# A ViT tower on one core: second feed-forward layer in blocks of 128 tokens with shared left-overs, output product of chosen rows once per two groups

## The chip, the cores and the metric

The kernel runs on one core of a Trainium2 chip. The engines of the core each work through a queue of their own in order: TensorE (PE, whose weight loads are shown as PEld), VectorE (DVE), ScalarE (ACT), GpSimd (POOL) and SyncE (SP, which here only issues transfers). The metric is the device time in microseconds (us) of one execution; less is better. Times of the kernel before: 670.09 us, median of 3 runs (669.08 to 673.85).

## The reference

The input x has shape (64, 12, 224, 224). Three stages follow one another.

1. Tokens: every 16x16 patch of each channel is summed, which gives 14x14 = 196 tokens of 12 numbers per image; a 12x192 matrix maps them to 192 features (h).
2. Attention on layernorm(h): 12 heads of 16, a causal mask, an output projection. Only k_sel = ceil(sqrt(196)) = 14 tokens per image, those with the largest softmax selection score, get the attention output added (`y = x.at[idx].add(gated attention)`); all others pass the layer norm itself. The result is added to h.
3. Feed-forward on layernorm(h): `gelu(xt @ in_weight.T + in_bias) @ out_weight`, with 192 -> 768 -> 192, added to h. The output has shape (64, 196, 192) in f32.

Because the tokens have rank 12 plus a constant, the kernel works with 12 to 13 numbers per token in place of 192 wherever the algebra allows.

## The kernel before, in words

Images go in groups of 4 (GB), 16 groups (NG). A group has 4 x 196 = 784 tokens (GT) and 4 x 14 = 56 chosen rows (SLOTS). Every engine runs the same loop over periods: in a period each stage works on the group given by the period's number less the stage's lag. The order inside a period is written out by hand, one string `plan` per engine (PE lines 724 to 727, ScalarE 908 to 910, DVE 1247, GpSimd 469); an entry such as `o:6.1:2` reads "stage o, step 6.1, lag 2". No scheduler moves anything; semaphores named by `Steps` (lines 99 to 107) order the engines among each other.

The stages, in the order in which a group passes them:

- **L** (DVE, line 1055): seven tiles of x are summed in the free dimension. For two tiles GpSimd adds halves first (H, line 430), for one a DMA adds them (X, line 425). The sums go through DRAM (ScalarE issues the store `R:st`, line 847, and the load `R:ld`, line 852) and come back by channel; GpSimd adds the quarters (line 439).
- **A**: token statistics and the selection. PE makes token products (`tm`, line 585), DVE the first layer norm's scale (line 1065 and on), PE transposes (`zt`, line 591, and `sl`, line 596, the scores of selection), DVE finds the top 14 (line 1113 to 1131; the last of it writes `srow`), PE turns `srow` (`st`, line 600), DVE makes the one-hot matrix Sg (line 1137).
- **K**: GpSimd (lines 373 to 467), in turns with ScalarE (line 830), splits the tokens into bf16 parts; PE transposes them (`tr1`, `tr2`, line 613) and ScalarE copies them out of PSUM as two stacks, `Stk1` (line 836, step k1) and `Stk2` (line 841, step k2). The copies also reorder the tokens so that block i holds tokens i, i+7, i+14, ...: `by_tile` and `tokens_by_tile`, lines 341 to 347.
- **f**: the first feed-forward layer, twelve bf16 products of 392 columns through the one PSUM bank psF (PE line 700), each followed by a GELU on ScalarE (line 893) that must end before the next product starts.
- **o / O**: the second layer. Seven blocks (FT) of 112 tokens (OT) per group, each six f32 products of 192 columns and one bf16 product for the residual (PE lines 715 and 719; an f32 product is two MATMUL instructions in the trace), evicted by ScalarE (line 900). After block 6 ScalarE issues the group's store (line 903). Two banks, psO, take turns.
- **G**: PE gathers the chosen tokens (`ga`, lines 624 to 626), DVE masks them (ZY, line 1145), PE makes U and the residual rows (`u`, lines 632 and 637), DVE masks U into UB (line 1162).
- **S**: attention of the chosen rows. Scores (PE 647), row maxima (DVE 1169), exponentials (ScalarE 864), reciprocal (DVE 1175), normalisation (ScalarE 869), transpositions (PE 653, ScalarE 873), product with the tokens (PE 659), mask into G2 (DVE 1180), the output product `at` (PE line 670: six f32 products of G2, 56 columns, with B2, 192 columns, in three lots of two) and the new rows h1 (DVE 1190).
- **C**: once per two groups, on the 120 rows of h1 (56 of the even group, 56 of the odd one from row 64 on): layer norm, both feed-forward layers (PE 679 to 690, ScalarE 879 to 887, DVE 1196 to 1211); then GpSimd writes the chosen rows over their places in the output by an indirect store (line 450), after the group's plain store has landed.

The entries that matter for the change, in PE's order within a period: `K:tr1 o:4.0 o:4.1 K:tr2 f:0 at:0 A:sl at:1 o:4.2 f:1 at:2 f:2 o:5.0 f:3 A:st o:5.1 f:4 G:ga f:5 o:5.2 f:6 G:u f:7 o:6.0 C:xt f:8 o:6.1 C:fa f:9 S:sc f:10 o:6.2 f:11 C:fb A:tm o:0.0`. The C entries act only where the group of lag 2 is odd. ScalarE's order at the period's end is `f:10 O:6 f:11 C:gb S:e0 ... S:e5`, then, in the next period, `O:0 S:n A:fm`.

Of the kernel before, what the change touches and what calls it, by code (L numbers as in the profile page):

```python
# [7 lines left out]
T = N * N  # L8
HD = D // HEADS
KSEL = int(np.ceil(np.sqrt(T)))  # L10
GB = 4
NG = B // GB
# [24 lines left out]
FT = 7  # L37
FP = T // FT
OT = GB * FP
# [70 lines left out]
def program(nc, x, cw, wqkv, bqkv, selw, selb, ow, ob, temp, w1t, b1, w2, consts, e48, e13r, out):  # L110
# [4 lines left out]
    og = out.rearrange("(g b) (t i) e -> g (b t) (i e)", b=GB, i=FT)  # L115
# [4 lines left out]
    with ExitStack() as ctx:  # L120
# [54 lines left out]
        act_sb = [sb(f"act{i}", [128, HT, GT]) for i in range(2)]  # L175

# [5 lines left out]
        G2 = sb("G2", [128, HP, SLOTS])  # L182
        dsm, dsel = sb("dsm", [SLOTS, GB]), sb("dsel", [SLOTS, 1])
        base = sb("base", [SLOTS, 1])
        idx = [sb(f"idx{i}", [SLOTS, 1], i32) for i in range(4)]
        res = sb("res", [SLOTS, D])
# [5 lines left out]
        obuf = [sb(f"obuf{i}", [OT, FT, D]) for i in range(2)]  # L192

# [24 lines left out]
        y_out = [sem(f"out_stored{k}") for k in range(2)]  # L218
        scat = [sem(f"chosen_stored{k}") for k in range(2)]
# [22 lines left out]
        pe_S = Steps(sem("pe_attention"), "sc et g at")  # L242
        dve_S = Steps(sem("dve_attention"), "mx nm ri g0 g1 h1")
        act_S = Steps(sem("act_attention"), "e0 e1 e2 e3 e4 e5 n0 n1 n2 n3 n4 n5 t0 t1 t2")

# [4 lines left out]
        outs = " ".join(f"o{k}" for k in range(FT))  # L250
        pe_F1 = Steps(sem("pe_ffn1"), ffn)
        act_F1 = Steps(sem("act_gelu"), ffn)
# [88 lines left out]
        def by_tile(t):  # L341

            return t[:, :].rearrange("p (i m) -> p i m", i=FT)

        def tokens_by_tile(ap):

            return ap.rearrange("p (m i) -> p i m", i=FT)
# [37 lines left out]
        def _(sp):  # L385
# [29 lines left out]
            for r in range(2):  # L415
                sp.wait_ge(sums_out[r], landed(NG - 4 + r, r))
                sp.wait_ge(y_out[r], landed(NG - 2 + r, r))
                sp.wait_ge(scat[r], landed(NG - 2 + r, r))

        @block.gpsimd  # L420
        def _(pool):
# [79 lines left out]
        def _(pe):  # L501
# [115 lines left out]
            def step_G(g, u, name):  # L617
# [46 lines left out]
            def step_at(g, j):  # L664

                if j == 0:
                    pe.wait_ge(dve_S.sem, dve_S.at(g, "g1"))
                    if isinstance(g, int) and g < 2:
                        pe.wait_ge(dve_W.sem, dve_W.at(0, "ob"))
                mm = pe.matmul(psS[0:SLOTS, 0, 0:D], G2[:, j, :], B2[:, j, :], start=(j == 0), stop=(j == HP - 1))  # L670
                if j == HP - 1:
                    mm.then_inc(pe_S.sem, 1)
# [30 lines left out]
            def step_F2(g, u, i, m):  # L703

                to = psO[(i + u) % 2][0:OT, 0:D]
                if m == 0:
# [5 lines left out]
                    if exists(g if i >= 2 else g - 1):  # L712
                        pe.wait_ge(act_F2.sem, act_F2.at(g if i >= 2 else g - 1, f"o{(i - 2) % FT}"))
                if m < HT:
                    pe.matmul(to, act_sb[u % 2][:, m, i * OT:(i + 1) * OT], W2[:, m, :], start=(m == 0), stop=False)  # L715
                else:
                    if i == 0:
                        pe.wait_ge(act_K.sem, act_K.at(g, "k2"))
                    pe.matmul(to, Stk2[u % 2][:, i * OT:(i + 1) * OT], RS[:, :], start=False, stop=True).then_inc(pe_F2.sem, 1)  # L719
# [9 lines left out]
            def body(i, k):  # L729
                for what in first if isinstance(i, int) and k == 1 else plan:  # L730
# [11 lines left out]
                    elif stage == "o":  # L742
                        for m in {0: (0, 1), 1: (2, 3), 2: (4, 5, 6)}[int(step[2])]:
                            step_F2(g, u, int(step[0]), m)
                    elif stage == "f":
                        step_F1(g, u, int(step))
                    elif stage == "at":
                        step_at(g, 2 * int(step))
                        step_at(g, 2 * int(step) + 1)
                    else:  # L750
                        {"A": step_A, "G": step_G, "K": step_K, "S": step_S}[stage](g, u, step)
# [8 lines left out]
        def _(act):  # L760
# [24 lines left out]
            def first_group():  # L785
# [21 lines left out]
                for name in "HML":  # L807
                    step_K(0, 0, name)
# [15 lines left out]
            def step_K(g, u, name):  # L824
# [7 lines left out]
                elif name == "k1":  # L832
# [3 lines left out]
                    act.activation(by_tile(Stk1[u % 2]), tokens_by_tile(psA[:, :].bitcast(bf16)[0:SK, 0:GT]), ACT.Copy).then_inc(act_K.sem, 1)  # L836
                else:
                    act.wait_ge(pe_K.sem, pe_K.at(g, "tr2"))
                    if exists(g - 2):
                        act.wait_ge(pe_F2.sem, pe_F2.at(g - 2, f"o{FT - 1}"))  # L840
                    act.activation(by_tile(Stk2[u % 2]), tokens_by_tile(psA[:, :].bitcast(bf16)[0:SK, 0:GT]), ACT.Copy).then_inc(act_K.sem, 1)
# [12 lines left out]
            def step_G(g, u, name):  # L854

                act.wait_ge(pe_G.sem, pe_G.at(g, "rs"))
                act.activation(res[:, :], psS[0:SLOTS, 0, D:2 * D], ACT.Copy).then_inc(act_G.sem, 1)
# [38 lines left out]
            def step_F2(g, u, i):  # L896
                act.wait_ge(pe_F2.sem, pe_F2.at(g, f"o{i}"))
                if i == 0 and exists(g - 2):
                    act.wait_ge(y_out[u % 2], landed(g - 2, u % 2))
                act.activation(obuf[u % 2][:, i, :], psO[(i + u) % 2][0:OT, 0:D], ACT.Copy).then_inc(act_F2.sem, 1)  # L900
                if i == FT - 1:
                    act.wait_ge(act_F2.sem, act_F2.at(g, f"o{i}"))
                    act.dma_start(og[bass.ds(g, 1)].rearrange("o p q -> (o p) q"),
                                  obuf[u % 2][:, :, :].rearrange("p i e -> p (i e)")).then_inc(y_out[u % 2], 16)

            first = ("K:k1:1 K:k2:1 f:0:1 f:1:1 f:2:1 f:3:1 f:4:1 f:5:1 f:6:1 f:7:1 f:8:1 f:9:1 f:10:1 f:11:1 "
                     "O:0:1 G:rs:1 O:1:1 S:e0:1 S:e1:1 S:e2:1 S:e3:1 S:e4:1 S:e5:1").split()
            plan = ("O:0:2 S:n:2 A:fm:1 O:1:2 A:e:1 S:t:2 K:H:1 K:M:1 O:2:2 K:L:1 K:k1:1 R:st:0 K:k2:1 f:0:1 O:3:2 "
                    "f:1:1 f:2:1 O:4:2 f:3:1 f:4:1 R:ld:0 f:5:1 O:5:2 f:6:1 f:7:1 G:rs:1 C:XH:2 f:8:1 f:9:1 C:ga:2 "
                    "f:10:1 O:6:2 f:11:1 C:gb:2 S:e0:1 S:e1:1 S:e2:1 S:e3:1 S:e4:1 S:e5:1").split()  # L910

            def body(i, k):
                for what in first if isinstance(i, int) and k == 1 else plan:
# [9 lines left out]
                    elif stage == "O":  # L923
                        step_F2(g, u, int(step))
                    elif stage == "f":
                        step_F1(g, u, int(step))
                    else:
                        {"A": step_A, "G": step_G, "K": step_K, "R": step_R, "S": step_S}[stage](g, u, step)
# [374 lines left out]
```

## Time and profile before

| | |
|---|---|
| median of 3 runs | 670.09 us |
| the profiled execution | 671.92 us, span 670.2 us |
| PE / PEld busy | 590.3 (88%) / 474.7 (71%) |
| DVE busy | 508.6 (76%) |
| ACT / POOL busy | 347.2 (52%) / 242.1 (36%) |
| mean granted clock of TensorE | 0.949 |
| transfers | 171.82 MB, mean 256 GB/s |
| the group's output store | x16, 588.0 KB each, 8.4 us from issue to landing |

The span runs from the first to the last instruction. "Busy" is the union of an engine's instruction times; a matmul's record is longer than the distance to the next one, since they are pipelined. In a row of a timeline the first number is the start in us, the second the length of the merged stretch, xN the number of instructions in it, and what stands in brackets is the idle time of the engine just before and who ended it.

### The profile page before, as it was taken

The numbers are of one execution on the slowest core, as the hardware profiler recorded it, in microseconds if no ns is written. First come the engines' busy times: TensorE is split into PE (matmuls) and PEld (weight loads), VectorE is DVE, ScalarE is ACT, GpSimd is POOL, SyncE is SP. The second block draws the span as 40 slices with busy tenths as digits, with TensorE's granted clock in tenths as the row PEclk, the third lists the DMA queues.
The fourth block names the chain that finished last, engine by engine and source line by source line (L and its number), as shares of the span: only waits on it lengthen the run. The fifth ranks groups of instructions, "written<-read, shape, count | busy, mean of one in ns | idle before, by whom it ended". The sixth has DMA issues, their size and how long they took to land.

```text
span 670.2 us, 12462 instructions
## 1 busy us (share of the span) xinstructions
PE 590.3 (88%) x3912; PEld 474.7 (71%) x3912; DVE 508.6 (76%) x1110; ACT 347.2 (52%) x847; POOL 242.1 (36%) x458
## 2 busy tenths in 40 slices
PE   2568687999998999899979979989989999999995
PEld 1346374777977797768767867769777877788774
DVE  4988669797979797979888866979897888752411
ACT  2013325475656556655656445656565565646541
POOL 1022333151545245443626224533634273304001
PEclk9886586999999999999999979999999999999998
DMA  8999958889898969897897869797999884010101
GB/s 320 332 384 366 400 160 326 288 289 309 283 354 277 353 231 366 266 358 243 322 308 282 260 229 295 256 355 240 361 271 342 257 334 95 10 41 12 32 6 42
DMA packets 33461, 171.82 MB, mean 256 GB/s; under 512 B 3428, under 2 KB 17776, under 8 KB 20978
## 3 DMA queue, kind: packets, MB, share of 16 engines
q1 hardware_dynamic: 21600, 146.11, 60.4%
q0 software_dynamic: 6512, 11.01, 9.1%
q10 hardware_dynamic: 5282, 13.87, 5.6%
q8 instruction: 34, 0.56, 0.3%
q14 instruction: 33, 0.27, 0.1%
HBM read 158.55 MB, written 12.43 MB: 255 GB/s over the span
## 4 chain that ended last, share of the span: by engine, by line
PE 44%; DVE 19%; issue 12%; DMA 9%; POOL 8%; ACT 5%; POOLq 1%; SPq 1%; DVEq 0%; ACTq 0%
PE psO L715 16%; DVE R L1055 5%; DMA X<-in_x 5%; PE psS L670 4%; PE psF L700 3%; PE psS L647 3%; DMA patch_sums<-R 3%; PE psS L659 3%; PE psC L685 2%; PE psC L690 2%; PE psA L613 2%; DMA out<-OS,idx 2%; DVE mx L1169 2%; PE psS L653 2%; ACT SP L830 1%
## 5 line engine op out<-in xcount | busy, mean ns | idle before, releaser
L715 PE MATMUL psO<-W,act 128*112 128x192 f32 x1344 | 266.6, 336 | 7.0 <-ACT act L893 7.0
L1055 DVE TENSOR_REDUCE R<-X 128x42 f32<-128x2688 f32 (+1 forms) x111 | 258.8, 2358 | 18.2 <-POOL X L430 16.6
L715 PEld LDWEIGHTS psO<-W,act 128*112 128x112 f32 x1344 | 217.4, 180 | 25.6 <-issue 17.8
L893 ACT ACTIVATE act<-psF 128x392 f32<-128x392 f32 x192 | 95.3, 497 | 134.8 <-PE psF L700 122.1
L430 POOL TENSOR_TENSOR X<-X 128x1344 f32<-128x1344 f32 x31 | 93.9, 3032 | 13.5 <-DMA X<-in_x 13.5
L700 PE MATMUL psF<-Stk,M1S 104*128 104x392 bf16 x192 | 65.9, 343 | 8.5 <-ACT act L893 8.5
L439 POOL TENSOR_TENSOR Pt<-Praw 48x196 f32<-48x196 f32 x14 | 7.5, 536 | 153.2 <-DMA Praw<-patch_sums 153.2
L900 ACT ACTIVATE obuf<-psO 112x192 f32<-112x192 f32 x112 | 36.6, 326 | 27.8 <-PE psO L719 23.4
L659 PE MATMUL psS<-ET,F 98*64 98x336 f32 x128 | 41.9, 472 | 1.5 <-ACT ET L873 1.5
L700 PEld LDWEIGHTS psF<-Stk,M1S 104*128 104x128 bf16 x192 | 18.9, 99 | 32.9 <-ACT act L893 24.8
L670 PE MATMUL psS<-B,G 128*56 128x192 f32 x192 | 41.0, 337 | 0.0
L864 ACT ACTIVATE Sm<-psS,nm 112x196 f32<-112x196 f32 x96 | 39.3, 429 | 2.9 <-DVE nm L1172 2.6
L869 ACT ACTIVATE Sm<-Sm,rinv 112x196 f32<-112x196 f32 x96 | 35.2, 445 | 5.4 <-DVE rinv L1175 5.2
L647 PE MATMUL psS<-FM,UB 120*112 120x196 f32 x192 | 35.2, 333 | 2.2 <-DVE UB L1162 1.0
L873 ACT ACTIVATE ET<-psS 98x448 f32<-98x448 f32 x48 | 22.6, 543 | 24.4 <-PE psS L653 24.4
L450 POOL DMA_INDIRECT out<-OS,idx x16 | 15.8, 988 | 51.6 <-DVE OS L1211 47.7
L647 PEld LDWEIGHTS psS<-FM,UB 120*112 120x112 f32 x192 | 31.1, 176 | 4.1 <-issue 3.7
L425 POOL DMA_DIRECT2D X<-in_x x15 | 21.4, 1426 | 33.8 <-DMA X<-in_x 33.7
L659 PEld LDWEIGHTS psS<-ET,F 98*64 98x64 f32 x128 | 16.8, 142 | 20.5 <-issue 5.6
L373 POOL TENSOR_SCALAR t<-y_ln 98x8 f32<-98x8 f32 x15 | 3.6, 241 | 75.8 <-DVE y_ln L1069 75.8
L830 ACT ACTIVATE SP<-d 98x624 bf16<-98x624 f32 (+1 forms) x32 | 20.7, 647 | 18.7 <-POOL d L464 10.8
L670 PEld LDWEIGHTS psS<-B,G 128*56 128x56 f32 x192 | 21.1, 129 | 13.0 <-issue 9.8
(225 smaller groups left out, 929.4 us busy)
## 6 DMA issues: line engine op xcount, KB each, us to landing
X<-in_x SPq DMA_DIRECT2D x96, 1344.0 KB, 8.0
X<-in_x SPq DMA_DIRECT2D x15, 672.0 KB, 4.4
X<-in_x POOLq DMA_DIRECT2D x15, 672.0 KB, 13.5
out<-obuf ACTq DMA_DIRECT2D x16, 588.0 KB, 8.4
patch_sums<-R ACTq DMA_DIRECT2D x14, 147.0 KB, 8.4
Praw<-patch_sums ACTq DMA_DIRECT2D x14, 147.0 KB, 5.5
act<-in_x SPq DMA_DIRECT2D x1, 1344.0 KB, 18.7
W1T<-in_w1t SPq DMA_DIRECT2D x1, 576.0 KB
```

Of the source, the lines that this page charges most:

```text
L430: pool.tensor_tensor(v[:, :, 0:2, :], v[:, :, 0:2, :], v[:, :, 2:4, :], ALU.add).then_inc(done[t], 1)
L647: mm = pe.matmul(psS[0:ROWS, j // 2, (j % 2) * T:(j % 2 + 1) * T], UB[:, j, :, :].rearrange("p k s -> p (k s)"), FM[r][:, :], start=True, ...
L659: mm = pe.matmul(psS[0:ZR, 1 + i, 0:3 * ROWS], F[r][:, k, 0:ZR], ET[:, k * HP + 3 * i:k * HP + 3 * i + 3, :].rearrange("p j s -> p (j s)") ...
L670: mm = pe.matmul(psS[0:SLOTS, 0, 0:D], G2[:, j, :], B2[:, j, :], start=(j == 0), stop=(j == HP - 1))
L700: pe.matmul(psF[:, 0:GT // 2], M1S[:, (n // 2) * 128:(n // 2 + 1) * 128], Stk1[u % 2][:, (n % 2) * (GT // 2):(n % 2 + 1) * (GT // 2)], sta ...
L715: pe.matmul(to, act_sb[u % 2][:, m, i * OT:(i + 1) * OT], W2[:, m, :], start=(m == 0), stop=False)
L830: act.activation(SP[:, :, n0:n1, :], src[:, :, :].unsqueeze(2).broadcast_to([HALF, 4 * GB, n1 - n0, W1]), ACT.Copy).then_inc(act_K.sem, 1)
L864: act.activation(Sm[:, j, :], psS[0:ROWS, j // 2, (j % 2) * T:(j % 2 + 1) * T], ACT.Exp, bias=nm[:, j:j + 1], accum_out=rsum[:, j:j + 1]). ...
L869: act.activation(Sm[:, j, :], Sm[:, j, :], ACT.Copy, scale=rinv[:, j:j + 1]).then_inc(act_S.sem, 1)
L893: act.activation(act_sb[u % 2][:, n // 2, (n % 2) * (GT // 2):(n % 2 + 1) * (GT // 2)], psF[:, 0:GT // 2], ACT.Gelu).then_inc(act_F1.sem, 1)
L900: act.activation(obuf[u % 2][:, i, :], psO[(i + u) % 2][0:OT, 0:D], ACT.Copy).then_inc(act_F2.sem, 1)
L1055: dve.tensor_reduce(R[:, r, t * TQ * N:(t + 1) * TQ * N].rearrange("p (q j) -> p q j", q=TQ), v, AX.XY, ALU.add).then_inc(dve_L, 1)
```

## The change

The second layer's blocks become 128 tokens wide, so that a group has 6 whole blocks (768 tokens) and 16 tokens are left. ScalarE copies the left tokens' GELU outputs and their part of the second stack beside those of the other group of the pair (`act_left`, `stk_left`), and a thirteenth block of 32 rows, which stands at step 6 of the odd group, computes them for both groups. In the even group step 6 is empty. The group's large store now follows block 5; the left-over rows go out by two small stores behind the thirteenth block. The output product `at` is made once per pair, from a G2 of 128 columns that holds both groups' rows; `dsel` and `res` likewise hold both, and h1 is written once for 120 rows. `ga` of an odd group waits for the even group's G2 in place of its h1. The indirect store also waits for the left-over stores.

```diff
-FT = 7
-FP = T // FT
-OT = GB * FP
+FT = GB * T // 128
+OT = 128
+WHOLE = FT * OT
+LEFT = GB * T - WHOLE
+NB = 2 * FT + 1
...
-    og = out.rearrange("(g b) (t i) e -> g (b t) (i e)", b=GB, i=FT)
+    og = out.rearrange("(g b) t e -> g (b t) e", b=GB)
...
+        def block_of(u, i):
+            return (u % 2) * FT + i
...
 def store_chosen(g, k, e, q):
                 pool.wait_ge(y_out[e], landed(g, e))
+                pool.wait_ge(y_left, q * 32 + 32)
...
 PE, step_G "ga":
-                    if exists(g - 1):
-                        pe.wait_ge(dve_S.sem, dve_S.at(g - 1, "h1"))
+                    if exists(g - 1) and u % 2:
+                        pe.wait_ge(dve_S.sem, dve_S.at(g - 1, "g1"))
+                    elif exists(g - 1):
+                        pe.wait_ge(dve_Q.sem, dve_Q.at(q - 1, "h1"))
...
-                mm = pe.matmul(psS[0:SLOTS, 0, 0:D], G2[:, j, :], B2[:, j, :], start=(j == 0), stop=(j == HP - 1))
+                mm = pe.matmul(psS[0:PROWS, 0, 0:D], G2[:, j, 0:PROWS], B2[:, j, :], start=(j == 0), stop=(j == HP - 1))
...
-            def step_F2(g, u, i, m):
-                to = psO[(i + u) % 2][0:OT, 0:D]
+            def step_F2(g, u, q, i, m):
+                j = block_of(u, i)
+                rows = OT if i < FT else 2 * LEFT
+                to = psO[(u // 2 + j) % 2][0:rows, 0:D]
...
+                    elif i == FT:
+                        pe.wait_ge(act_F1.sem, act_F1.at(g, "left"))
+                    if j >= 2:
+                        pe.wait_ge(act_F2.sem, act_F2.at(q, f"o{j - 2}"))
...
+                    rows_in = act_sb[u % 2][:, m, i * OT:(i + 1) * OT] if i < FT else act_left[:, m, u // 2, :]
...
                         for m in {0: (0, 1), 1: (2, 3), 2: (4, 5, 6)}[int(step[2])]:
-                            step_F2(g, u, int(step[0]), m)
+                            if u % 2 or int(step[0]) < FT:
+                                step_F2(g, u, pair_of(i, k, lag), int(step[0]), m)
...
                     elif stage == "at":
-                        step_at(g, 2 * int(step))
-                        step_at(g, 2 * int(step) + 1)
+                        if u % 2:
+                            step_at(g, pair_of(i, k, lag), 2 * int(step))
+                            step_at(g, pair_of(i, k, lag), 2 * int(step) + 1)
...
+            def copy_stack(to, left):
+                tokens = psA[:, :].bitcast(bf16)[0:SK, 0:GT]
+                act.activation(by_block(to), tokens_by_block(tokens), ACT.Copy)
+                act.activation(left, tokens[:, WHOLE:GT], ACT.Copy).then_inc(act_K.sem, 1)
...
+            def gather_left(g, u):
+                act.wait_ge(act_F1.sem, act_F1.at(g, f"n{NF1 - 1}"))
+                at = LEFT * (u % 2)
+                act.activation(act_left[:, :, u // 2, at:at + LEFT], act_sb[u % 2][:, :, WHOLE:GT], ACT.Copy).then_inc(act_F1.sem, 1)
...
 ScalarE, step_F2:
+                if i == FT:
+                    if exists(g - 2):
+                        act.wait_ge(y_left, q * 32)
+                    act.activation(out_left[:, :], bank[0:2 * LEFT, 0:D], ACT.Copy).then_inc(act_F2.sem, 1)
...
+                if i >= FT - 1:
+                    act.wait_ge(act_F2.sem, act_F2.at(q, f"o{j}"))
                 if i == FT - 1:
...
+                elif i == FT:
+                    for e in range(2):
+                        act.dma_start(left_of(g - 1 + e), out_left[e * LEFT:(e + 1) * LEFT, :]).then_inc(y_left, 16)
...
-                    "f:10:1 O:6:2 f:11:1 C:gb:2 S:e0:1 S:e1:1 S:e2:1 S:e3:1 S:e4:1 S:e5:1").split()
+                    "f:10:1 O:6:2 f:11:1 C:gb:2 l:0:1 S:e0:1 S:e1:1 S:e2:1 S:e3:1 S:e4:1 S:e5:1").split()
...
+                dve.memset(G2[:, :, :], 0.0)
+                dve.memset(dsel[:, :], 0.0)
+                dve.memset(res[:, :], 0.0)
...
-                    dve.wait_ge(pe_S.sem, pe_S.at(g, "at"))
+                    dve.wait_ge(pe_Q.sem, pe_Q.at(q, "at"))
                     dve.wait_ge(act_G.sem, act_G.at(g, "rs"))
-                    dve.scalar_tensor_tensor(out=h1[r:r + SLOTS, :], in0=psS[0:SLOTS, 0, 0:D], scalar=dsel[:, 0:1], in1=res[:, :],
-                                             op0=ALU.mult, op1=ALU.add).then_inc(dve_S.sem, 1)
+                    dve.scalar_tensor_tensor(out=h1[:, :], in0=psS[0:PROWS, 0, 0:D], scalar=dsel[:, 0:1], in1=res[:, :],
+                                             op0=ALU.mult, op1=ALU.add).then_inc(dve_Q.sem, 1)
...
+                        if step != "at" or u % 2:
+                            stage_S(g, u, step, pair_of(i, k, lag))
```

## Rows read from the trace of the kernel before

**Rows 1.** Busy time by stretch: PE, PEld, DVE, ACT, POOL, then clock, DMA share, GB/s.
```profile
247.20:280.00 32.80, 30.93 (x211) 24.78 (x210) 28.64 (x55) 20.13 (x50) 16.28 (x29) 1.00 0.94 317
280.00:317.40 37.40, 35.87 (x247) 29.74 (x248) 31.11 (x76) 21.82 (x55) 15.24 (x32) 1.00 0.85 289
```

**Rows 2.** Timeline of GpSimd: first variance step of three periods, and the last of v.
```profile
246.07 0.23 POOL L373 TENSOR_SCALAR t<-y_ln 98x8 f32<-98x8 f32 x1 [6.46 <-DVE y_ln L1069]
...
252.44 0.35 POOL L461 TENSOR_TENSOR v<-v,y_ln 98x96 f32<-98x96 f32 x1
...
279.84 0.24 POOL L373 TENSOR_SCALAR t<-y_ln 98x8 f32<-98x8 f32 x1 [3.47 <-DVE y_ln L1069]
...
316.38 0.23 POOL L373 TENSOR_SCALAR t<-y_ln 98x8 f32<-98x8 f32 x1 [6.05 <-DVE y_ln L1069]
```

**Rows 3.** Timeline of PE in the even period and its end.
```profile
259.88 0.33 PE L596 MATMUL psA<-K,TS 98*4 98x98 f32 x2
...
261.75 0.33 PE L700 MATMUL psF<-Stk,M1S 104*128 104x392 bf16 x1
...
264.00 0.50 PE L600 MATMUL psA<-K,srow 4*98 4x4 f32 x4
...
269.29 0.34 PE L700 MATMUL psF<-Stk,M1S 104*128 104x392 bf16 x1
...
270.22 0.34 PE L700 MATMUL psF<-Stk,M1S 104*128 104x392 bf16 x1
...
279.99 0.33 PE L591 MATMUL psA<-K,F 98*64 98x98 f32 x2 [0.96 <-DVE lr L1094]
```

**Rows 4.** Timeline of ScalarE: even period, and the end of the odd one.
```profile
249.35 0.21 ACT L817 ACTIVATE Ex<-Dm 98x16 f32<-98x16 f32 x1
...
252.91 0.73 ACT L830 ACTIVATE SP<-v 98x624 bf16<-98x624 f32 x1
...
259.00 0.82 ACT L841 ACTIVATE Stk<-psA 104x784 bf16<-104x784 bf16 x1 [0.92 <-PE psA L613]
259.84 1.28 ACT L893 ACT_TABLE_LOAD   x1
...
311.61 0.33 ACTq L903 DMA_DIRECT2D out<-obuf  x1
312.05 0.50 ACT L893 ACTIVATE act<-psF 128x392 f32<-128x392 f32 x1 [0.60 <-ACT obuf L900]
```

**Rows 5.** Timeline of DVE: even period, and the reciprocal of the odd one.
```profile
258.73 1.55 DVE L1055 TENSOR_REDUCE R<-X 128x42 f32<-128x1344 f32 x1 [0.88 <-POOL X L430]
...
263.40 0.35 DVE L1131 TENSOR_TENSOR srow<-cum,mask 4x196 f32<-4x196 f32 x1
...
267.22 2.93 DVE L1055 TENSOR_REDUCE R<-X 128x42 f32<-128x2688 f32 x1
270.08 0.90 DVE L1162 TENSOR_TENSOR UB<-psS,K 64x336 f32<-64x336 f32 x2
...
273.77 1.36 DVE L1169 TENSOR_REDUCE mx<-psS 112x6 f32<-112x1176 f32 x1
...
316.86 0.18 DVE L1175 RECIPROCAL rinv<-rsum 112x6 f32<-112x6 f32 x1
```

**Rows 6.** Chain of waits in order of time, with a block and a product lot.
```profile
252.12 1.32 PE psO L715 x8
...
255.84 0.83 PE psO L715 x4
...
259.05 0.79 PE psS L670 x4
```

**Rows 7.** Timeline at the end, PE: softmax transpositions of the last group.
```profile
641.46 1.36 PE L653 MATMUL psS<-K,Sm 112*98 112x112 f32 x12 [0.67 <-ACT Sm L869]
```

**Rows 8.** Busy time by stretch early in the span, columns as in rows 1.
```profile
84.00:89.00 5.00, 3.22 (x21) 2.07 (x20) 3.65 (x16) 1.99 (x4) 1.42 (x1) 1.00 0.82 189
89.00:93.00 4.00, 3.92 (x14) 3.59 (x14) 3.61 (x16) 0.00 (x0) 2.04 (x10) 0.57 0.01 4
```

More of the change, by code:

```diff
@@ L175, in program @@
         act_sb = [sb(f"act{i}", [128, HT, GT]) for i in range(2)]
+        act_left, stk_left = sb("act_left", [128, HT, 2, 2 * LEFT]), sb("stk_left", [SK, 2, 2 * LEFT], bf16)
         ZY = sb("ZY", [FR, SLOTS])
@@ L249, in program @@
         ffn = " ".join(f"n{k}" for k in range(NF1))
-        outs = " ".join(f"o{k}" for k in range(FT))
+        outs = " ".join(f"o{k}" for k in range(NB))
         pe_F1 = Steps(sem("pe_ffn1"), ffn)
-        act_F1 = Steps(sem("act_gelu"), ffn)
+        act_F1 = Steps(sem("act_gelu"), ffn + " left")
         pe_F2 = Steps(sem("pe_ffn2"), outs)
@@ L718, in step_F2 @@
                         pe.wait_ge(act_K.sem, act_K.at(g, "k2"))
-                    pe.matmul(to, Stk2[u % 2][:, i * OT:(i + 1) * OT], RS[:, :], start=False, stop=True).then_inc(pe_F2.sem, 1)
+                    rows_in = Stk2[u % 2][:, i * OT:(i + 1) * OT] if i < FT else stk_left[:, u // 2, :]
+                    pe.matmul(to, rows_in, RS[:, :], start=False, stop=True).then_inc(pe_F2.sem, 1)
             first = ("K:tr1:1 K:tr2:1 f:0:1 A:sl:1 f:1:1 f:2:1 f:3:1 f:4:1 f:5:1 f:6:1 f:7:1 P:1:0 A:st:1 f:8:1 "
@@ L835, in step_K @@
                         act.wait_ge(pe_F1.sem, pe_F1.at(g - 2, f"n{NF1 - 1}"))
-                    act.activation(by_tile(Stk1[u % 2]), tokens_by_tile(psA[:, :].bitcast(bf16)[0:SK, 0:GT]), ACT.Copy).then_inc(act_K.sem, 1)
+                    copy_stack(Stk1[u % 2], Stk1[u % 2][:, WHOLE:GT])
                 else:
@@ L923, in body @@
                     elif stage == "O":
-                        step_F2(g, u, int(step))
+                        if u % 2 or int(step) < FT:
+                            step_F2(g, u, pair_of(i, k, lag), int(step))
+                    elif stage == "l":
+                        gather_left(g, u)
+                    elif stage == "K":
+                        step_K(g, u, pair_of(i, k, lag), step)
                     elif stage == "f":
@@ L927, in body @@
                     else:
-                        {"A": step_A, "G": step_G, "K": step_K, "R": step_R, "S": step_S}[stage](g, u, step)
+                        {"A": step_A, "G": step_G, "R": step_R, "S": step_S}[stage](g, u, step)
             weights()
@@ L1156, in stage_G @@
                     dve.wait_ge(dve_G.sem, dve_G.at(g, "dm"))
[L1157 removed]
+                    dve.tensor_reduce(dsel[ODD * (u % 2):ODD * (u % 2) + SLOTS, :], dsm[:, :], AX.X, ALU.add).then_inc(dve_G.sem, 1)
                     dve.tensor_scalar(base[:, :], base[:, :], float(GT), None, ALU.add).then_inc(dve_G.sem, 1)
@@ L1263, in body @@
                             weights_bias()
-                        stage_S(g, u, step, pair_of(i, k, lag))
+                        if step != "at" or u % 2:
+                            stage_S(g, u, step, pair_of(i, k, lag))
                     elif stage == "C":
```

73 lines of the change are left out of this document (41 added, 32 removed).

## The prediction

> **What bounds the kernel now.** I read the engines' busy time by stretch first. An even period (the stretch in which PE works on the output blocks of an even group) lasts 32.80 us with PE busy for 30.93 and DVE for 28.64; an odd one 37.40 with 35.87 and 31.11 [rows 1]. PE has the least slack, and a reader who stops here takes the change for a gain. So I asked next what recurs once per period and whom it waits for. GpSimd's first variance step starts at 246.07, 279.84 and 316.38 us: an even period is 33.8 long, an odd one 36.5, a pair 70.3 [rows 2].
>
> Following one even period through the queues gives a loop in which PE is only one link: GpSimd's step at 246.07, its chain of small operations up to v at 252.44+0.35 = 252.79 [rows 2], ScalarE's split copy at 252.91, again GpSimd and ScalarE in turn, the halving of an x tile, DVE's sum of it at 258.73 (it had waited 0.88 for GpSimd), top-14 selection ending with srow at 263.40+0.35 = 263.75, PE's turn of it at 264.00, then DVE without a hole: x sum at 267.22, UB at 270.08, a second x sum, the row maxima at 273.77 [rows 3 to 5]. PE is served 0.25 us after srow is ready, and at the period's end PE itself sits idle 0.96 us for DVE [rows 3]. The pair is near-balanced: PE is nearly full and also nearly always just behind something else.
>
> **What is removed from PE.** Of 14 blocks per pair of groups 13 remain. Eight matmuls of a block take 1.32 us, so 12 take 1.98; the four that end a block take 0.83, which puts the bf16 product and its change of weights at about 0.1: 2.1 us per block [rows 6]. The product G·B2 runs once per pair instead of twice: three lots of four at 0.79 = 2.4 us [rows 6]. That is 4.5 us per pair, 36 us in 8 pairs. Both savings lie in even periods; in an odd period PE still has seven blocks, one product (120 columns of weights instead of 56, the moving side stays 192), and the chosen rows' FFN. I cost the wider weights at nothing, since loads run beside the matmuls; a wider load behind which PE waits would cost at most as much as the saved block's excess.
>
> **Where it would show, place by place in the even period.**
> First lots of the product, around the transposition of the selection (sl). PE starts sl at 259.88, right behind ScalarE's copy of the second stack, which ends at 259.00+0.82 = 259.82 [rows 3, 4]. Taking the product away in front of it moves nothing. Behind it, the second first-layer product (261.75) needs the first GELU, and that comes after the table load 259.84+1.28 = 261.12 and a GELU of 0.5: 261.6 [rows 3, 4]. Gain at most 0.1. The third lot stands between two first-layer products, whose distance is a GELU and two hand-overs: 0.93 us from 269.29 to 270.22, also where PE had another 0.8 us of work between them [rows 3]. Gain 0.1. Then srow: 264.00 cannot become earlier than 263.8. So 2.4 us of removed product are worth 0.2 at most, and the x sum ahead of the selection, which waits for GpSimd, fixes that.
> Seventh block. Its three parts stand between first-layer products 8, 9 and 12, where the GELU distance of 0.93 holds with or without 0.8 us of filler [rows 3]. Worth 0.1 to 0.2, and the next consumer, DVE, is busy until 273.77 in any case [rows 5]. What PE finishes sooner it waits for at the period's end, where it already waits 0.96 [rows 3]. I count both together as 0, bounds 0 and 1.0 us per pair gained (the upper end if the loop shortens by each hand-over margin of about 0.25 four times).
>
> **What is added, all on ScalarE.** (a) Each stack copy becomes two, the small one of 16 columns. The nearest row is a 16-element operation of 0.21; behind another one it shows less [rows 4]. Two per group. The one at stack 1 is hidden by PE's block work; the one at stack 2 delays sl by 0.1 to 0.2, and sl ends at 260.21, where DVE comes free of its x sum at 260.28 [rows 3, 5]. Cost 0.1 in an even period; in an odd one about 0.1 through the table load and PE's full queue.
> (b) The gather of 6x16 columns per group behind the twelfth GELU: between the same 0.21 and a stack copy's 0.82, nearest 0.21, I take 0.3 with the wait for its own engine. In even periods the seventh copy and a store vanish ahead of it, and nothing is lost.
> (c) In odd periods two small stores (12 KB each) stand where one of 588 KB stood, ahead of the twelfth GELU; an issue takes 0.33 [rows 4]. The GELU at 312.05 starts 0.35 later, the exponentials 0.6 later. Behind them wait DVE's reciprocal (316.86), which delays DVE 0.45, covered by its 0.88 of waiting at the next x sum, and PE's first block of the next group [rows 4, 5]. PE's shift of 0.3 reaches the transpositions of the softmax and then ScalarE's split copy, which has 252.91-252.79 = 0.12 of margin [rows 2, 4]: 0.2 to 0.3 on the loop.
> (d) The large store is issued one block sooner, behind ScalarE's wait for its own copy; queued behind it is a GELU that PE needs only after the U products. Nothing, if the read of the patch sums just before it on the same queue isn't slowed; this bound is 0 to 0.5.
> (e) Even h1 on DVE goes (0.4) where DVE then waited for PE: nothing. Three memsets at the start, about 960 elements at 2.93/2688 us each [rows 5], 1 us, stand ahead of DVE's wait for the constants, which I take as their cover: nothing, at most 1. GpSimd waits for the left-over stores three periods after they were issued: nothing; only for the last pair up to 0.5.
>
> **Sum.** +0.3 in the even and +0.1 in the odd part of a pair, +0.4 times 7 pairs that run in full, +2.8. In the last even period there are no x sums, and PE's softmax transposition at 641.46 waited 0.67 for ScalarE [rows 7]; ScalarE is freed there of 0.6 and given 0.3: -0.4. Total +2.4. The profiled execution took 671.9 (span 670.2), which stands 1.8 above the median of 670.1; against itself it gives 674.3, against the median **672.5**. Bounds: -1.0 to +1.2 per pair, 662 to 680; the forecast's own range is 668 to 678.
>
> **Rivals.**
> *PE sets the pace.* For it: PE's busy share [rows 1]. If all 4.5 us counted: 634. Against it: every place above. If a quarter to a third counts, because PE's earlier arrival lets hand-overs close up in odd periods too: 12 us, 658. Chance 0.22.
> *PE's clock falls in the thinned stretches.* This one ends slower. From 84 to 89 us PE was busy for 3.22 of 5.00 us, first-layer products with a GELU between them, at 2.4 GHz (granted 1.00); in the next 4 us the granted clock is 0.57, mostly 1.2 GHz [rows 8]. After the change the even period has such a stretch: sl, a block's last part and three first-layer products, 2.2 us of records in 4.0; and another behind the U products, two GELU distances with nothing between. In periods as they are the clock is 1.00. It decides if the fall comes: the scores product, 12 matmuls, 2.0 us, would start when UB is ready, at 271.0 to 271.3, take 4.0 and end 1.6 after the 273.77 at which DVE turns to it [rows 5]; the products that pick the chosen tokens stand on the loop too, for which I add half of that, 0.8 (an estimate). 2.4 times 8 = 19, 689; in half of the periods 680. Against it: the stretches are shorter than 5 us and dense work lies on both sides. Chance 0.18. The Trainium skill, "TensorE: Matmul & The Clock Gate", in its section on a second failure mode, says that many small idle gaps between groups of matmuls can make the gate swing between its levels; by that rule this rival is the outcome. The trace agrees for 84 to 93 us only.
> *Nothing of it shows.* The copies hide, savings hide: 670, chance 0.08, within the forecast's range.
> The forecast itself has 0.52.
>
> **Numbers.** A measurement here can tell about 1% from no change, 663.4 to 676.8. Faster by more: nearly all of the first rival, 0.21. Slower: most of the clock rival, 0.16, and the forecast's upper end, 0.10: 0.26. Same: 0.53. Range for 8 in 10: down to 658, which leaves out about half of the first rival, up to 684, which leaves out the clock rival's worse half.
>
> **What would show it.** PE busy per even period down by some 4 us with the period still 33.5 to 34.3 between GpSimd's steps; PE's idle ahead of first-layer products, of the srow products and at the period's end up by as much; the odd period 36.5 to 36.9; ScalarE's table load for the exponentials about 0.6 later in odd periods. I am wrong if even periods fall below 33, if the granted clock of the stretch from 259 to 275 is below 1.00, or if the read of the patch sums lands later and the token products follow it.

## The result and the profile after

The changed kernel takes 714.49 us (median of 4 runs, 707.34 to 718.22) against 671.97 for the kernel before (4 runs): ratio 1.059, 95% interval 1.054 to 1.064. It is slower by 42.5 us, where 672.5 was predicted with 658 to 684 as the range. The execution whose profile is read below took 718.22 us, the slowest of the four, and the ratio leaves it out, so the profile shows a little more of the loss than the median run has. Work left PE as planned, and the clock under it fell.

The page of the changed kernel: busy time and, by slices of the span, the granted clock in tenths (of 2.4 GHz; the lower level, 1.2 GHz, is 5).

```profile
span 716.5 us, 12155 instructions
PE 616.1 (86%) x3712; PEld 488.2 (68%) x3712; DVE 504.3 (70%) x1105; ACT 351.8 (49%) x887; POOL 242.1 (34%) x458
PEclk9885685699999995899689999999588975999598
```

PE executes 200 matmul instructions fewer than before and is busy 26 us longer. The slices with 5 to 8 outside the first 130 us are new; the kernel before had a single one there, a 7 where its loop turns (385 to 402 us), and an 8 at its very end. The mean clock went from 0.949 to 0.859. At two levels that means 0.282 of 716.5 us = 202 us at 1.2 GHz against 0.102 of 670.2 = 68 us: 134 us more.

GpSimd's first variance step marks the periods again, and the stretches between are the periods (columns as in rows 1). Odd and even ones alternate, beginning with an odd one:

```profile
145.04:181.40 36.36, 35.06 (x240) 28.14 (x241) 30.43 (x73) 21.78 (x57) 14.72 (x29) 1.00 0.85 292
181.40:215.71 34.31, 29.82 (x193) 23.85 (x191) 28.47 (x58) 20.88 (x54) 16.91 (x32) 0.95 0.88 308
215.71:252.18 36.47, 35.03 (x239) 28.10 (x240) 30.36 (x73) 21.67 (x57) 14.79 (x29) 1.00 0.85 294
252.18:293.48 41.30, 37.32 (x191) 30.06 (x190) 28.64 (x59) 21.35 (x56) 16.90 (x31) 0.71 0.76 258
293.48:330.39 36.91, 35.28 (x243) 28.35 (x242) 30.26 (x72) 21.08 (x54) 14.74 (x29) 1.00 0.83 286
330.39:370.54 40.15, 35.51 (x195) 28.51 (x193) 28.70 (x58) 21.24 (x57) 16.93 (x31) 0.79 0.78 266
...
407.07:445.57 38.50, 32.83 (x206) 26.66 (x205) 28.70 (x59) 22.44 (x61) 16.88 (x31) 0.93 0.84 277
445.57:484.34 38.77, 36.08 (x238) 28.41 (x239) 30.44 (x73) 21.28 (x55) 14.73 (x30) 0.96 0.80 275
484.34:525.88 41.54, 37.65 (x193) 30.40 (x193) 28.69 (x59) 21.61 (x59) 16.93 (x32) 0.71 0.75 257
525.88:566.06 40.18, 37.86 (x241) 29.51 (x240) 30.31 (x73) 20.88 (x53) 14.77 (x29) 0.92 0.76 264
566.06:607.66 41.60, 37.72 (x194) 30.51 (x193) 28.65 (x59) 21.68 (x59) 16.97 (x32) 0.71 0.48 156
```

The odd periods up to 407 us are as before, 36.4 to 36.9 against 36.5 [rows 2]. An even period with the clock nearly whole (0.95) takes 34.3 where 33.8 was measured before; with the clock at 0.71 it takes 41.3 to 41.6, with 0.79 40.2. Most of the loss is in even periods with a low clock, but not all: set beside the periods of the kernel before in the same places, the seven even ones are 33.0 us longer together, the seven odd ones 7.2 (3.8 of it in the one from 525.88, where the clock is 0.92), and what lies outside them 6.1, together the 46.3 us between the spans.

Inside the even period from 252.18 the fall can be dated (same columns, shorter stretches):

```profile
261.00:265.00 4.00, 4.00 (x32) 3.10 (x31) 3.29 (x4) 1.85 (x5) 3.58 (x2) 1.00 1.01 427
265.00:269.00 4.00, 1.86 (x15) 1.04 (x12) 3.09 (x9) 3.36 (x6) 3.48 (x3) 0.97 1.01 411
269.00:273.00 4.00, 3.92 (x14) 3.28 (x15) 1.56 (x5) 1.24 (x4) 0.00 (x0) 0.50 1.04 363
273.00:280.00 7.00, 7.00 (x42) 6.12 (x41) 3.92 (x7) 1.82 (x4) 1.12 (x3) 0.50 0.89 225
280.00:286.00 6.00, 4.82 (x16) 3.21 (x15) 3.77 (x3) 1.82 (x4) 3.52 (x2) 0.50 0.85 265
286.00:292.00 6.00, 5.41 (x18) 4.11 (x17) 3.37 (x11) 3.48 (x9) 0.00 (x0) 0.50 0.47 199
292.00:296.00 4.00, 4.00 (x26) 3.82 (x25) 3.72 (x14) 3.70 (x16) 1.73 (x8) 0.92 0.00 0
```

From 265 to 269 PE is busy 1.86 of 4.00 us; then the clock is 0.50 and stays there for more than 23 us, through work that looks full (7.00 of 7.00), until the next group's first block. PE's timeline shows what stands there, and which wait thins it (start, length, line, tiles, count, idle before and its releaser):

```profile
265.10 0.33 PE L719 MATMUL psF<-Stk,M1S 104*128 104x392 bf16 x1
266.33 0.33 PE L613 MATMUL psA<-K,TS 98*4 98x98 f32 x2 [0.90 <-ACT stk_left L879]
266.50 0.84 PE L741 MATMUL psO<-W,act 128*128 128x192 f32 x4
...
268.15 0.34 PE L719 MATMUL psF<-Stk,M1S 104*128 104x392 bf16 x1 [0.72 <-ACT act L931]
269.07 0.51 PE L719 MATMUL psF<-Stk,M1S 104*128 104x392 bf16 x1 [0.59 <-ACT act L931]
269.38 1.49 PE L741 MATMUL psO<-W,act 128*128 128x192 f32 x4
...
281.96 0.51 PE L719 MATMUL psF<-Stk,M1S 104*128 104x392 bf16 x1 [0.59 <-ACT act L931]
283.06 0.51 PE L719 MATMUL psF<-Stk,M1S 104*128 104x392 bf16 x1 [0.59 <-ACT act L931]
283.36 4.14 PE L666 MATMUL psS<-FM,UB 120*112 120x196 f32 x12
```

The second first-layer product starts 3.05 us after the first (268.15 against 265.10), and in the kernel before it was 3.03 (261.75 [rows 3] against this one):

```profile
258.72 0.33 PE L700 MATMUL psF<-Stk,M1S 104*128 104x392 bf16 x1
```

Two lots of the output product used to stand in between. The product at 269.07 already takes 0.51 instead of 0.34. Four f32 instructions take 1.49 instead of 0.81, the scores product 4.14 instead of 2.24. DVE waits for it: over the span its row maxima waited 35.9 us for the scores product, 10.7 before.

The same thin stretch stands in every even period, but the clock does not fall behind it in every one. In the even period from 181.40 PE is busy for 1.88 of 4.00 us and the clock stays at 1.00, and so it does in the one from 407.07 (1.78 of 4.00); in the four from 252.18, 330.39, 484.34 and 566.06 (1.86 to 2.12) the next four us have 0.50. In the first two the clock falls later, behind the U products, and for 3 to 4 us only. The first of them:

```profile
194.50:198.50 4.00, 1.88 (x11) 1.24 (x11) 3.07 (x10) 3.38 (x6) 3.22 (x3) 1.00 1.00 389
198.50:202.50 4.00, 4.00 (x30) 3.31 (x28) 2.00 (x8) 2.21 (x5) 0.00 (x0) 1.00 1.02 359
```

What decides between the two outcomes, no run here shows.

### The profile page after: what moved, and what is told of

The parts are those of the page before. It is cut to its first block, busy times and chain, and to the rows that moved or that the text cites. A ratio compares the mean times of both kernels' runs of the same rounds, so it can differ in the third digit from the quotient of the medians.

```text
span 716.5 us, 12155 instructions
## 1 busy us (share of the span) xinstructions
PE 616.1 (86%) x3712; PEld 488.2 (68%) x3712; DVE 504.3 (70%) x1105; ACT 351.8 (49%) x887; POOL 242.1 (34%) x458
## 4 chain that ended last, share of the span: by engine, by line
PE 55%; DVE 10%; ACT 10%; DMA 8%; issue 8%; POOL 6%; ACTq 1%; SPq 1%; POOLq 1%; DVEq 0%
PE psO L741 19%; PE psS L666 6%; PE psF L719 6%; DMA X<-in_x 4%; DMA patch_sums<-R 4%; ACT act L931 4%; PE psS L651 4%; PE psS L678 3%; PE psC L709 2%; PE psA L630 2%; PE psC L704 2%; PE psS L672 2%; ACT L931 1%; DVE R L1119 1%; ACT SP L861 1%
## 5 line engine op out<-in xcount | busy, mean ns | idle before, releaser
L741 PE MATMUL psO<-W,act 128*128 128x192 f32 x1152 | 243.6, 355 | 4.9 <-ACT act L931 4.2
L741 PEld LDWEIGHTS psO<-W,act 128*128 128x128 f32 x1152 | 203.0, 205 | 19.1 <-issue 13.6
L719 PE MATMUL psF<-Stk,M1S 104*128 104x392 bf16 x192 | 76.6, 399 | 31.9 <-ACT act L931 31.6
L666 PE MATMUL psS<-FM,UB 120*112 120x196 f32 x192 | 47.4, 413 | 0.6 <-issue 0.4
L1233 DVE TENSOR_REDUCE mx<-psS 112x6 f32<-112x1176 f32 x16 | 22.1, 1378 | 35.9 <-PE psS L666 35.9
L666 PEld LDWEIGHTS psS<-FM,UB 120*112 120x112 f32 x192 | 42.3, 230 | 3.2 <-issue 1.5
L952 ACT ACTIVATE obuf<-psO 128x192 f32<-128x192 f32 x96 | 31.2, 325 | 23.6 <-PE psO L746 23.3
L878 ACT ACTIVATE Stk<-psA 104x768 bf16<-104x768 bf16 x32 | 26.0, 811 | 32.1 <-PE psA L630 32.1
L651 PEld LDWEIGHTS psS<-ZY,A 64*64 64x64 f32 x384 | 31.3, 171 | 4.6 <-issue 4.6
L651 PE MATMUL psS<-ZY,A 64*64 64x56 f32 x384 | 33.7, 258 | 0.0
L441 POOL DMA_DIRECT2D X<-in_x x15 | 21.4, 1425 | 34.1 <-DMA X<-in_x 34.0
```

The costliest lines, as they stand in the source:

```text
L651: mm = pe.matmul(psS[0:ZR, 1 + h // HP, (h % HP) * SLOTS:(h % HP + 1) * SLOTS], A4[:, h, :], ZY[0:ZR, :], start=True, stop=True)
L666: mm = pe.matmul(psS[0:ROWS, j // 2, (j % 2) * T:(j % 2 + 1) * T], UB[:, j, :, :].rearrange("p k s -> p (k s)"), FM[r][:, :], start=True, ...
L719: pe.matmul(psF[:, 0:GT // 2], M1S[:, (n // 2) * 128:(n // 2 + 1) * 128], Stk1[u % 2][:, (n % 2) * (GT // 2):(n % 2 + 1) * (GT // 2)], sta ...
L741: pe.matmul(to, rows_in, W2[:, m, :], start=(m == 0), stop=False)
L878: act.activation(by_block(to), tokens_by_block(tokens), ACT.Copy)
L952: act.activation(obuf[u % 2][:, i, :], bank[0:OT, 0:D], ACT.Copy).then_inc(act_F2.sem, 1)
```

## The experiments

All ratios are against the kernel before, measured beside it on the same chip; its median lay between 671.36 and 671.90 us each time. "Idle product" is `fill`, a product of a 128-column weight tile with 192 columns of W2 into a part of psC that nobody reads; the outputs stay as they are.

**1. The product alone.** The parts of the diff that merge `at`, G2, `dsel`, `res` and h1, with the blocks as before.

```diff
+                        if u % 2:
+                            step_at(g, pair_of(i, k, lag), 2 * int(step))
+                            step_at(g, pair_of(i, k, lag), 2 * int(step) + 1)
...
 FT = 7
```

> One part alone: the kernel before, its seven blocks of 112 kept, with only the output product (and h1) made once per two groups. Theory C (the clock): thinned PE work in even periods lets TensorE's clock fall to 1.2 GHz, and that is the whole loss. Only the stretch around the first three first-layer products is thinned here, so the clock falls less often than with both parts: mean granted clock 0.88 to 0.95, ratio to before 1.00 to 1.04. Rival A (ScalarE's added copies and stores and the moved store lengthen the loop): none of them is in this kernel, ratio 0.99 to 1.00, clock 0.95.

Measured: 697.95 us, 1.031 (1.025 to 1.037), clock 0.889, within the range of theory C. Rival A is out for this part: ScalarE does nothing new here and half of the loss is there. Two even periods and the odd one behind the second:

```profile
180.91:214.32 33.41, 29.69 (x205) 24.51 (x203) 28.93 (x58) 21.02 (x53) 16.90 (x31) 1.00 0.95 313
...
250.40:290.31 39.91, 36.89 (x205) 30.92 (x203) 28.51 (x59) 19.90 (x48) 16.85 (x31) 0.79 0.83 287
290.31:327.06 36.75, 34.84 (x243) 29.39 (x242) 30.36 (x73) 22.19 (x58) 14.70 (x29) 1.00 0.80 269
```

Six f32 products fewer, and the even period from 250.40 is 6 us longer than before, at a clock of 0.79. The one from 180.91 kept its clock at 1.00 and took 33.41, with PE busy for 29.69; in the kernel before, the period in the same place took 33.71 with 31.94.

**2. The blocks alone.** All other parts of the diff; the product once per group. (The first two lines below are against the kernel before, the rest against the changed one.)

```diff
+FT = GB * T // 128
+OT = 128
...
-                        if u % 2:
-                            step_at(g, pair_of(i, k, lag), 2 * int(step))
+                        step_at(g, 2 * int(step))
```

> The other part alone: blocks of 128 with the left-over block, the output product again once per group. Theory C: the stretch behind the U products is thinned, the scores product falls into it; clock 0.88 to 0.95, ratio 1.01 to 1.05. Rival A: all added ScalarE work and the moved stores are here, so nearly all of the loss, 1.05 to 1.06, at whatever clock.

Measured: 679.83 us, 1.012 (1.009 to 1.015), clock 0.939. All of ScalarE's added work and the moved stores are in this kernel, so 1.2% bounds what they cost, less whatever the missing block saves. Part of it is still the clock, 0.95 in this even period:

```profile
247.04:282.43 35.39, 32.88 (x210) 26.17 (x208) 28.92 (x60) 21.55 (x58) 16.91 (x32) 0.95 0.86 302
282.43:319.09 36.66, 35.27 (x238) 27.28 (x239) 30.37 (x72) 21.46 (x56) 14.68 (x30) 1.00 0.83 289
```

The two parts alone give 1.031 and 1.012, both together in one kernel 1.059: more than the sum.

**3. Idle work in all the former places.** The changed kernel with 12 idle products per even period.

```diff
+            def fill(n):
+                for m in range(n):
+                    pe.matmul(psC[:, 256:256 + D], W2[:, m % HT, 0:128], W2[:, m % HT, :], start=True, stop=True)
...
+                        if u % 2 == 0 and int(step[0]) == FT:
+                            fill(2)
...
+                        else:
+                            if step == "0" and exists(g - 2):
+                                pe.wait_ge(dve_C.sem, dve_C.at(pair_of(i, k, lag) - 1, "os1"))
+                            fill(2)
```

> The changed kernel, with PE's lost work put back as idle work: in even periods two f32 products of 128x192 that nobody reads stand at each of the three places of the output product and at each of the three places of block 6 (12 products in all). Theory C: clock back at 0.94 or more, ratio to before 1.00 to 1.01 (ScalarE's additions, 2 to 4 us, remain). Rival A: ScalarE's work is as in the changed kernel, ratio 1.04 or more.

Measured: 674.6 us, 1.0024 (0.9995 to 1.0053), clock 0.955. Both are as theory C had them. This is the deciding run: with ScalarE's work, the stores and the merged product all kept, PE given work that serves nothing brings 40 us back. (The wait in front of the first idle product, in the diff, is for DVE's last read of psC.)

```profile
244.86:278.76 33.90, 31.96 (x218) 26.48 (x216) 29.17 (x59) 21.72 (x57) 16.89 (x32) 1.00 0.89 312
278.76:316.02 37.26, 33.70 (x232) 27.06 (x233) 30.33 (x72) 19.67 (x46) 14.72 (x29) 1.00 0.82 287
```

The even period has clock 1.00 and 33.90 us, where it was 33.77 before the change.

**4. The same work in another place.** Six idle products in one piece at the end of each even period.

```diff
-                    "f:9:1 S:sc:1 f:10:1 o:6.2:2 f:11:1 C:fb:2 A:tm:0 o:0.0:1 o:0.1:1 o:0.2:1 C:f2:2 o:1.0:1").split()
+                    "f:9:1 S:sc:1 f:10:1 o:6.2:2 f:11:1 C:fb:2 A:tm:0 o:0.0:1 o:0.1:1 o:0.2:1 C:f2:2 o:1.0:1 X:e:2").split()
...
+                    elif stage == "X":
+                        if u % 2 == 0:
+                            fill(6)
```

> Control: the changed kernel with six such products in one piece at the end of each even period, where PE waits for DVE. Theory C with the place deciding: the thin stretches stay thin, clock 0.85 to 0.89, ratio 1.05 to 1.07. If the total of PE's work decided and not the place, the clock would rise to 0.92 or more and the ratio fall to 1.03 or less. Rival A: 1.06.

Measured: 716.48 us (700.02 to 729.44, 4 runs) against 671.42; the spread was too wide for an interval. The profiled run took 708.63, at a clock of 0.892. Even the fastest of the four is 4.3% above the kernel before, where 3% at most was expected if the total of PE's work decided. The idle products here are half of those of experiment 3; experiment 7 has as many as this one and settles it. Here an odd period suffers as well.

```profile
258.66:298.87 40.21, 36.23 (x188) 29.27 (x187) 28.64 (x59) 21.39 (x56) 16.86 (x32) 0.73 0.77 265
298.87:338.76 39.89, 38.49 (x257) 31.64 (x257) 30.51 (x72) 21.13 (x54) 14.70 (x29) 0.97 0.78 265
```

**5 and 6. One of the two thin stretches filled.** `fill(2)` only at the product's places, then only at block 6's.

> The changed kernel with idle products (two at a time) only at the three places of the output product in even periods; the places of block 6 stay empty. Theory C with both thin stretches counting: the product stretch is filled, what is left is as in the kernel with blocks only, so ratio 1.01 to 1.02, clock 0.93 to 0.95.

> The changed kernel with idle products only at the three places of block 6 in even periods; the places of the output product stay empty. Theory C: what is left is as in the kernel with the product only, ratio 1.02 to 1.04, clock 0.88 to 0.92. If instead filling any one of the two stretches were enough, this and its sister would both be below 1.01.

Measured: product's places filled 676.67 us, 1.006 (1.003 to 1.009), clock 0.932; block 6's places filled 697.87 us, 1.032 (1.023 to 1.041), clock 0.906. The second is what was expected and what the product alone gave (1.031). The first lies below the expected 1.01 to 1.02 and below the 1.012 of the blocks alone; the intervals just meet. So the stretch of the first three first-layer products, where the output product stood, is the one whose thinning costs most; the other adds to it.

**7. Half the idle work.** `fill(1)` at all six places.

> One idle product instead of two at each of the six places (6 in all, as many as in the control at the period's end, but spread). Theory C: if the fall is a matter of how thin the stretch is, this holds the clock mostly: ratio 1.00 to 1.03, well below the control's 1.07. If only the full former work holds it: 1.04 or more.

Measured: 670.45 us, 1.0002 (0.9969 to 1.0036), clock 0.957. As many idle products as in experiment 4, spread over the thin stretches instead of in one piece: the total of PE's work isn't what counts, its place is. The page shows no slice below 9 after the first seven:

```profile
PEclk9796586999999999999999999999999999999999
```

and PE's timeline shows the stretch of the fall with its small fillers (L751); the distance of the first-layer products at 258.85 and 261.90 is again 3.05:

```profile
258.85 0.33 PE L719 MATMUL psF<-Stk,M1S 104*128 104x392 bf16 x1
259.02 0.49 PE L751 MATMUL psC<-W 128*128 128x192 f32 x2
260.09 0.33 PE L613 MATMUL psA<-K,TS 98*4 98x98 f32 x2 [0.58 <-ACT stk_left L890]
260.25 0.52 PE L751 MATMUL psC<-W 128*128 128x192 f32 x2
260.61 0.81 PE L741 MATMUL psO<-W,act 128*128 128x192 f32 x4
...
261.90 0.34 PE L719 MATMUL psF<-Stk,M1S 104*128 104x392 bf16 x1 [0.39 <-ACT act L942]
```

**8 and 9. The left-over block as real filler.** It moves one period later, into step 6 of the next even group; one version with GpSimd's order as it is, one with its indirect store of the chosen rows behind the halving of tile 5 and one idle product per place instead of two.

```diff
-                            if u % 2 or int(step[0]) < FT:
+                            if int(step[0]) < FT:
                                 step_F2(g, u, pair_of(i, k, lag), int(step[0]), m)
+                            else:
+                                left_block(g, u, pair_of(i, k, lag), m)
...
-            plan = ("c:s:5 X:3:1 P:s:2 H:5:1 A:var2:2 K:v:2 K:d1:2 K:d2:2 H:0:0").split()
+            plan = ("X:3:1 P:s:2 H:5:1 c:s:5 A:var2:2 K:v:2 K:d1:2 K:d2:2 H:0:0").split()
```

> A version for use: the left-over block is computed one period later, at step 6 of the next even period (for the last pair at the end), so that real work fills this place and the odd period has six blocks; idle products stand at the three places of the output product. Theory C: clock 0.94 or more and ratio 0.99 to 1.005; the 2 us less of PE work in odd periods, the copy and the stores moved out of them, give up to 0.5 us per pair where DVE waited for the token products. If the odd period is now the thin one, its clock falls and the ratio is above 1.02.

> The left-over block one period later, as before, but GpSimd's indirect store of the chosen rows stands behind the halving of tile 5 in GpSimd's order instead of first, and one idle product instead of two stands at each place of the output product. In the trace of the first version GpSimd waited up to 24 us for the left-over store before that indirect store. Theory W (that wait was the loss): ratio 0.99 to 1.01, clock 0.94 or more. Rival C2 (odd periods are now the thin ones and their clock falls): ratio 1.03 or more with GpSimd's wait gone and low clock in odd periods.

Measured: 754.1 us, 1.124 (1.117 to 1.131), clock 0.895, and 735.04 us, 1.097 (1.092 to 1.103), clock 0.894. Both miss their expectations. The loss of the first is in the even periods, which hold the moved block and the idle products: 47.5 to 48.8 us each from 178 to 568 us, against 36.4 to 38.2 for the odd ones. The waits of the first version (who waited for what: us in total, times, longest):

```profile
POOL out L471 <- DMA out<-out_left: 93.8, 4, 24.0
DVE F L1176 <- PE psA L606: 85.0, 15, 14.1
PE psA L606 <- POOL P L463: 74.1, 6, 13.6
```

GpSimd's indirect store waits for the left-over rows, issued late in the even period; behind it in GpSimd's queue stand the patch sums' quarters, behind these PE's token products, behind these DVE. I had costed this wait at nothing because the left-over store comes long before. In the change it does; with the block one period later it doesn't. The second version still shows `POOL out <- DMA out<-out_left` with 39.7 us, and its low clock remains. The wait went from 93.8 to 39.7 us and the time from 754 to 735, but the number of idle products changed as well, and how much of the loss is the wait and how much the clock was not separated. That the wait is a large part is argued, not shown.

**10 and 11. The product alone, with three idle products.** The product merged, the blocks as before, `fill(1)` at each of the three former places; then the same kernel in five rounds.

> The kernel with the product only, plus one idle product at each of its three former places in even periods. Theory C: the fall is gone, and since none of ScalarE's additions are here, ratio 0.995 to 1.002, clock 0.945 or more. If the merged product cost something by itself (its wait, the wider weights), it would stay above 1.01 with the clock up.

> The same kernel as the run before it (product once per pair, one idle product at each of its three former places), in five rounds, to tell whether it is a version that beats the kernel before. If the gain is real: 0.995 to 0.999 with the whole interval below 1. If it was scatter: the interval takes in 1.

Measured: 668.65 us, 0.997 (0.994 to 1.000), and 668.43 us, 0.994 (0.991 to 0.997), clock 0.946 and 0.949. Three idle products per even period turn 1.031 into 0.997 and 0.994. The interval of the first takes in 1, that of the second doesn't: this version is faster than the kernel before by 0.3 to 0.6%, with single runs that overlap (665.48 to 670.18 against 667.24 to 677.17 in the second set).

Put together, from the profiled execution of each kernel (time at 1.2 GHz is twice one less the clock, times the span):

| kernel | span | clock | us at 1.2 GHz | over before | span over before |
|---|---|---|---|---|---|
| before | 670.2 | 0.949 | 68 | | |
| blocks only | 676.0 | 0.939 | 82 | 14 | 5.8 |
| product's places filled | 674.6 | 0.932 | 92 | 23 | 4.4 |
| block 6 filled | 698.2 | 0.906 | 131 | 63 | 28.0 |
| product only | 699.0 | 0.889 | 155 | 87 | 28.8 |
| idle products at the end | 706.9 | 0.892 | 153 | 84 | 36.7 |
| after | 716.5 | 0.859 | 202 | 134 | 46.3 |

Each added us at 1.2 GHz costs 0.19 to 0.44 us of span in these rows, and the kernels also differ in other work. A cost below 0.5 fits a PE slowed to half whose delay hides in part behind GELUs and DVE; that is an argument, no run separates it.

## Why the prediction was wrong

**The step that failed** is what the forecast charged for the clock. Its sum has no term for it: the fall was left to a rival with a chance of 0.18, at 2.4 us per even period, 689 in all if it came in every one, on the ground that "the stretches are shorter than 5 us and dense work lies on both sides". The runs show the fall behind the first thin stretch in four of the six even periods from 181 to 608 us, and 6 to 8 us for each (40.2 to 41.6 against 33.8), so even the rival at its worst stands 25 us short of the measured 714.49. I charged the slow clock for the scores product and half as much again for the gather. It lasted 17 to 24 us, and everything on the loop in that time is slower: the turn of srow, the gather of the chosen tokens, U, the scores and, in three of the four periods, the token products. The prediction's own sign of being wrong, a clock below 1.00 between 259 and 275 us, came in its place: 0.50 from 269 on.

That the fall would come was harder to tell. For it stood [rows 8]: 3.22 of 5.00 us, then 0.57. But the same trace also had stretches as thin behind which nothing fell, and the prediction says of these periods only that their clock is 1.00:

```profile
275.00:280.00 5.00, 3.17 (x21) 2.68 (x20) 4.45 (x20) 4.52 (x15) 1.53 (x2) 1.00 0.94 287
280.00:285.00 5.00, 5.00 (x38) 4.87 (x39) 4.93 (x8) 3.55 (x12) 3.25 (x16) 1.00 0.64 212
```

From 205 to 210 it is 3.13 of 5.00, from 347 to 352 2.95, each followed by 1.00. Ahead of srow, PE had been busy for 3.96 of 4.00 us (259.07 to 263.07), and the change made 1.86 of 4.00 out of it (2.2 was forecast). What I named as evidence against, that the new stretches are shorter, was an assumption without a row.

**The rest of the sum held where the clock holds.** With the clock restored the changed kernel gives 1.0024 and 1.0002 (experiments 3 and 7) where I had +2.4 us, 1.0036. Experiment 3 gives PE nearly all of its work back and so tests only what was added; experiment 7 gives back half of it: PE is busy for 573.5 us against 590.3, and the 17 us less bought nothing. The even period of experiment 1 that kept its clock says the same: 2.2 us less of PE's work, 0.3 us gained. The second first-layer product stands 3.05 us behind the first with or without filler, because it waits for the GELU, whose table load comes first. PE's idle time ahead of first-layer products went from 8.5 to 31.9 us, as the prediction named it. The rival "PE sets the pace" is out.

**ScalarE's additions** were priced about right. The 16-column copies take 0.18 each (0.1 to 0.2 forecast), the gather 0.29 (0.3). The two small stores take 0.83 together, 0.5 over one; the timeline of the odd period's end:

```profile
325.14 0.32 ACT L950 ACTIVATE out_left<-psO 32x192 f32<-32x192 f32 x1 [0.44 <-PE psO L746]
325.62 0.83 ACTq L960 DMA_DIRECT2D out<-out_left  x2
326.56 0.50 ACT L931 ACTIVATE act<-psF 128x392 f32<-128x392 f32 x1 [1.10 <-issue]
```

From the start of the stores to the GELU it is 0.94 where it was 0.44 [rows 4]: 0.50 later, and I had 0.35. PE waited 0.90 for the copies of the second stack ahead of sl at 266.33, in the stretch where the clock fell. Most of that is the stack copy itself: in experiment 1, which has no small copy, PE waited 0.83 there, and the clock fell all the same.

**The stores.** The large store lands in 4.8 us at the median where it took 8.4 (6.3 in experiment 7, where the clock holds); the read of the patch sums 5.1 where it took 5.5. The feared collision did not come.

**The rule on small gaps.** The prediction weighed a rule of the Trainium skill, "TensorE: Matmul & The Clock Gate", section "A second HAM failure mode: psum-queue depth-cycling": short idle gaps between groups of matmuls, if frequent enough, make the gate swing between its levels. The trace agrees: in the even period shown the clock went 1.00, 0.50 and back, with the longest idle time of PE in front of the fall at 0.90 us. It also shows that such gaps don't bring the fall each time, as above. So the chance of 0.18 was too low for what came, but it alone isn't the mistake: with the rival taken as the forecast, its 19 us would still be less than half of the 42.5 measured.

## What to carry to other kernels

Work taken from PE beside a chain that something else paces bought nothing here, and cost 5.9%. Look at what is left between the products of such a chain. If such a stretch was ever followed by a lower granted clock in the trace, give the fall a price of its own: here everything on the loop ran slow for 17 to 24 us, not one product. For the chance, look as well for stretches as thin that no fall followed. A cheap test is an idle product or two at the places of the removed work: if that raises the granted clock and makes the kernel faster, the clock was the loss. And read the clock before the busy share: PE's rose by 26 us with 200 instructions fewer. Where a transfer is waited for by an in-order queue, recount the periods in between whenever its producer moves.

## What the runs showed that I had not expected

The slow clock held on. From 269 to 292 us it was 0.50, with PE's records covering 7.00 of 7.00 us from 273 to 280, and not even the scores product raised it, 12 f32 instructions in 4.14 us; it rose within the next group's first block (12 f32 instructions from 289.82 on). In the even period from 330.39 it did rise within the scores product, 17 us after the fall. And very little is enough to keep it up: one idle product at each of three places, 0.5 us each in the records, removed a 3.1% loss. Why the product merged with filler comes out 0.3 to 0.6% faster than the kernel before stays open; its odd and even periods are as long as before (36.8 and 34.1 from 245.15 to 316.02), so the gain isn't in the steady pair that was looked at.
